# A fused four-block kernel: all four softplus in front of the scans and on VectorE, silus ahead of the last exponentials, first pair ahead in the norms

## What is computed

```python
x = x + _L0_conv_ref(_gn(x), ...)      # five steps of a diffusion
x = x + _L1_conv_ref(_gn(x), ...)      # 3x3 convolution
x = x + _L2_conv_ref(_gn(x), ...)      # layer norm, Mamba block, layer norm, projection
x = x + _L3_conv_ref(_gn(x))           # DCT

# inside _L2: mamba_block
xi, z = jnp.split(x @ in_proj_w.T, 2, axis=-1)
xs = silu(causal_conv(xi) + conv_b)
dt, Bm, Cm = jnp.split(xs @ x_proj_w.T, [dt_rank, dt_rank + d_state], axis=-1)
delta = softplus(dt @ dt_proj_w.T + dt_proj_b)
h = exp(delta * A) * h + (delta * xs) * B      # scan over 1024 pixels, per state
y = sum_n(h * C) + xs * D
y = y * silu(z)
```

## Time and profile before

| | us |
|---|---|
| median of 3 runs | 901.21 |
| lowest and highest | 901.0, 903.37 |
| the profiled execution's own time | 899.3 |
| its span | 897.5 |
| DVE busy | 792.5 (88%) |
| PE busy | 729.4 (81%) |
| ACT busy | 560.2 (62%) |
| POOL busy | 519.5 (58%) |

### The profile page before, as it was taken

How to read it: one execution, slowest core, us unless ns; L and a number is a source line. 1 busy time by engine, 2 the same in 40 slices (tenths; PEclk the granted TensorE clock), 3 DMA queues, 4 the chain that set the end, 5 groups by cost and what they waited for, 6 DMA issues and landing times.

```text
span 897.5 us, 10547 instructions
## 1 busy us (share of the span) xinstructions
PE 729.4 (81%) x3866; PEld 499.1 (56%) x3866; DVE 792.5 (88%) x682; ACT 560.2 (62%) x960; POOL 519.5 (58%) x243
## 2 busy tenths in 40 slices
PE   3898898977777678788799789988768677878896
PEld 2343343443677567778654434434338566777783
DVE  6979997769999998999969989775999999989984
ACT  2973342237669898979486724223684977897932
POOL 3104997121489697778510299912047979878851
PEclk9999999999789999999999999999988999999999
DMA  4002000000635355355200210000033445545431
GB/s 114 0 15 80 0 1 0 0 1 6 184 123 185 139 179 189 137 188 184 75 1 0 75 43 0 0 1 1 0 106 131 159 160 186 194 157 186 157 105 24
DMA packets 34066, 78.20 MB, mean 87 GB/s; under 512 B 15704, under 2 KB 15840, under 8 KB 34016
## 3 DMA queue, kind: packets, MB, share of 16 engines
q1 hardware_dynamic: 32608, 76.23, 25.3%
q0 software_dynamic: 320, 1.05, 0.5%
q10 hardware_dynamic: 1088, 0.26, 0.1%
HBM read 70.71 MB, written 2.62 MB: 82 GB/s over the span
## 4 chain that ended last, share of the span: by engine, by line
DVE 31%; PE 30%; ACT 20%; issue 13%; POOL 2%; DMA 1%; SPq 1%; DVEq 0%; POOLq 0%; ACTq 0%
ACT arena L958 15%; PE ps L749 7%; PE ps L510 6%; DVE arena L1775 6%; DVE ps L1766 5%; PE ps L549 4%; DVE HS L1775 3%; DVE arena L1730 3%; PE ps L763 2%; PE ps L641 2%; ACT ROWS L958 1%; ACT ps L958 1%; PE ps L600 1%; POOL arena L397 1%; PE ps L663 1%
## 5 line engine op out<-in xcount | busy, mean ns | idle before, releaser
L397 POOL TENSOR_TENSOR arena<-arena 128x1024 f32<-128x1024 f32 x85 | 200.3, 2368 | 60.9 <-DVE arena L1775 55.1
L958 ACT ACTIVATE arena<-arena 128x128 f32<-128x128 f32 (+3 forms) x412 | 157.0, 455 | 82.4 <-DVE arena L1669 64.7
L1775 DVE TENSOR_TENSOR_SCAN arena<-arena,ps 128x1024 f32<-128x1024 f32 x86 | 194.7, 2277 | 10.6 <-ACT arena L958 5.7
L958 ACT ACTIVATE arena<-arena,Amat 128x1024 f32<-128x1024 f32 x128 | 143.0, 1142 | 7.2 <-DVE arena L1775 6.0
L641 PE MATMUL ps<-mat,arena 128*128 128x128 f32 x1016 | 138.1, 281 | 5.5 <-POOL arena L397 5.0
L600 PE MATMUL ps<-mat,arena 128*128 128x128 f32 x560 | 82.2, 295 | 61.9 <-DVE arena L1775 35.9
L641 PEld LDWEIGHTS ps<-mat,arena 128*128 128x128 f32 x1016 | 119.7, 146 | 9.5 <-POOL arena L397 7.5
L397 POOL TENSOR_TENSOR arena<-HS,arena 128x1024 f32<-128x1024 f32 x42 | 99.6, 2370 | 30.1 <-DVE HS L1775 21.5
L749 PE MATMUL ps<-arena,mat 128*128 128x512 f32 x240 | 106.9, 595 | 9.4 <-DVE arena L1642 9.4
L600 PEld LDWEIGHTS ps<-mat,arena 128*128 128x128 f32 x560 | 66.8, 148 | 76.2 <-DVE arena L1775 45.3
L1775 DVE TENSOR_TENSOR_SCAN HS<-arena,ps 128x1024 f32<-128x1024 f32 x42 | 95.7, 2277 | 2.4 <-ACT arena L958 1.7
(11 more groups left out here) (219 smaller groups left out, 1321.8 us busy)
## 6 DMA issues: line engine op xcount, KB each, us to landing
arena<-c_rows SPq DMA_DIRECT2D x128, 512.0 KB, 3.9
arena<-arena SPq DMA_DIRECT2D x16, 252.0 KB
out<-arena SPq DMA_DIRECT2D x28, 64.0 KB, 2.4
xres<-x POOLq DMA_DIRECT2D x4, 256.0 KB, 5.4
xres<-x SPq DMA_DIRECT2D x4, 256.0 KB, 4.1
convw<-conv_w SPq DMA_DIRECT2D x1, 576.0 KB
c_rows<-ROWS SPq DMA_DIRECT2D x4, 128.0 KB, 1.9
mat<-mats SPq DMA_DIRECT2D x1, 448.0 KB, 3.9
```

The lines of the kernel that those rows point to most:

```text
L397: tt(HC[s % 2], HS[s % 3], CB[s % 4], ALU.mult).then_inc(S("hc"), 1)
L958: return nc.scalar.activation(out_, in_, func, bias=bias, scale=scale, accum_out=accum_out)
L1775: nc.vector.tensor_tensor_scan(HS[s % 3], DA[s % 3], PS[q][:, :], 0.0, ALU.mult, ALU.add).then_inc(S("scan"), 1)
```

## The change

- POOL: `relu_part` goes, all three of its calls a half.
- DVE: `relu_part(h, j)` takes the place of `first_relu_part` for all four images, and the semaphores are renumbered to suit. `normalize(0)` stands ahead of pair 1's statistics. `causal` takes a list of taps; `causal(0,0)` runs through, `variance(1)` behind it, two taps of `causal(0,1)` ahead of `normalize(1)` and two behind. `relu_x(1,1)`, `one_plus(3)` and `delta(3)` move in front of scan 0.
- PE: 14 spins behind the first group mean of the convolution. `xn_channels(0)` and `x_in_proj(0,0)` move ahead, the 4 spins between go. `dt_proj(0,0)` stands ahead of `xn_channels(1)`, and `z_in_proj(1,1)` and `dt_proj(1,1)` ahead of `bc_proj(0)`.
- ACT: `layer_scale(0)` ahead of `norm2(1)`, `abs_x(0,0)` ahead of `layer_scale(1)`. All silus stand ahead of `exp_of(2)`; `abs_x(1,1)` and `exp_of(3)` ahead of the logarithms, and the four logarithms stand together.

```diff
--- before.py
+++ after.py
@@ -379,12 +379,6 @@
 
-            def relu_part(h, j):
-                pool.wait_ge(S("sp"), 4 * h + j + 1)
-                pool.wait_ge(S(f"rx{j // 2}"), 2 * h + j % 2 + 1)
-                du = two_images(j, "DU")
-                tt(du, du, two_images(j, "DL"), ALU.subtract).then_inc(S("spw"), 1)
-
             def delta_u(h, j):
...
@@ -449,15 +443,11 @@
 
-                relu_part(h, 1)
-                relu_part(h, 2)
                 for s in range(SCANS):
...
                         delta_u(h, 1)
-                    if s == 5:
-                        relu_part(h, 3)
                     if s in (10, 25):
...
@@ -616,7 +606,7 @@
                 if j == 0:
-                    pe.wait_ge(S("first_du"), 2 * h + 2)
+                    pe.wait_ge(S("first_du"), h + 1)
                 else:
...
@@ -765,6 +755,7 @@
                 group_mean(D[0], h, 1, 0)
+                spin(PS[1], 14)
                 wino_product(h, 0, 0)
...
@@ -778,21 +769,22 @@
 
+                xn_channels(h, 0)
                 group_mean(D[1], h, 2, 1)
-                spin(PS[1], 4)
-                xn_channels(h, 0)
+                x_in_proj(h, 0, 0)
                 n2_pixels(h, 1)
-                x_in_proj(h, 0, 0)
                 z_in_proj(h, 0, 0)
                 x_in_proj(h, 0, 1)
+                dt_proj(h, 0, 0)
                 xn_channels(h, 1)
-                dt_proj(h, 0, 0)
                 x_in_proj(h, 1, 0)
...
                 z_in_proj(h, 0, 1)
+                z_in_proj(h, 1, 1)
+                dt_proj(h, 1, 1)
                 bc_proj(h, 0)
...
@@ -800,8 +792,6 @@
                 b_rows(h, 1)
-                z_in_proj(h, 1, 1)
-                dt_proj(h, 1, 1)
                 bc_proj(h, 1)
...
@@ -1309,35 +1299,35 @@
                 square(h, 0, 0)
+                layer_scale(h, 0)
                 norm2(h, 1)
-                layer_scale(h, 0)
                 square(h, 1, 0)
...
                 silu_x(h, 0, 0)
+                abs_x(h, 0, 0)
                 layer_scale(h, 1)
-                abs_x(h, 0, 0)
                 silu_x(h, 0, 1)
...
                 exp_of(h, 1)
+                abs_x(h, 1, 0)
                 silu_z(h, 0, 1)
-                abs_x(h, 1, 0)
+                silu_x(h, 1, 1)
+                silu_z(h, 1, 1)
                 exp_of(h, 2)
                 keep_rows(h, 0)
+                abs_x(h, 1, 1)
+                exp_of(h, 3)
                 ln_of(h, 0)
-                ln_of(h, 1)
                 keep_first_b(h)
-                ln_of(h, 2)
-                silu_x(h, 1, 1)
-                silu_z(h, 1, 1)
+                for j in range(1, 4):
+                    ln_of(h, j)
                 decay(h, 0)
...
                 keep_rows(h, 1)
-                abs_x(h, 1, 1)
                 decay(h, 2)
-                exp_of(h, 3)
                 decay(h, 3)
...
@@ -1355,8 +1345,6 @@
                         scaled_input(h, s + 3)
-                    if s == D_STATE - 1:
-                        ln_of(h, 3)
                     if h + 1 < HALVES:
...
@@ -1717,18 +1705,19 @@
 
-            def causal(h, k, b, first=True, rest=True):
+            def causal(h, k, b, some):
                 d, i = D[k], 2 * h + b
-                dve.wait_ge(S(f"xi{k}"), i + 1)
-                if b == 1:
-                    dve.wait_ge(S(f"xs{k}"), i)
                 w = [vecs[:, V_CONVW + t:V_CONVW + t + 1] for t in range(4)]
-                if first:
-                    ts(d["XI"], x_ps(k, b)[:, :], w[3], None, ALU.mult).then_inc(S(f"cconv{k}"), 1)
-                for t in range(1, 4) if rest else []:
-                    dve.wait_ge(S(f"cconv{k}"), 4 * i + t)
-                    stt(d["XI"][:, t:L], x_ps(k, b)[:, 0:L - t], w[3 - t], d["XI"][:, t:L], ALU.mult, ALU.add)\
-                        .then_inc(S(f"cconv{k}"), 1)
+                for t in some:
+                    if t == 0:
+                        dve.wait_ge(S(f"xi{k}"), i + 1)
+                        if b == 1:
+                            dve.wait_ge(S(f"xs{k}"), i)
+                        ts(d["XI"], x_ps(k, b)[:, :], w[3], None, ALU.mult).then_inc(S(f"cconv{k}"), 1)
+                    else:
+                        dve.wait_ge(S(f"cconv{k}"), 4 * i + t)
+                        stt(d["XI"][:, t:L], x_ps(k, b)[:, 0:L - t], w[3 - t], d["XI"][:, t:L], ALU.mult, ALU.add)\
+                            .then_inc(S(f"cconv{k}"), 1)
 
...
@@ -1743,17 +1732,14 @@
                 dve.wait_ge(S("ln"), 4 * h + j + 1)
-                if j == 0:
-                    dve.wait_ge(S("first_du"), 2 * h + 1)
-                else:
-                    dve.wait_ge(S("spw"), 3 * h + j)
+                dve.wait_ge(S("spw"), 4 * h + j + 1)
                 tt(two_images(j, "DL"), UU[j], two_images(j, "DU"), ALU.add).then_inc(S("delta"), 1)
 
-            def first_relu_part(h):
-                du = two_images(0, "DU")
-                dve.wait_ge(S("sp"), 4 * h + 1)
-                dve.wait_ge(S("rx0"), 2 * h + 1)
-                tt(du, du, two_images(0, "DL"), ALU.subtract).then_inc(S("first_du"), 1)
+            def relu_part(h, j):
+                du = two_images(j, "DU")
+                dve.wait_ge(S("sp"), 4 * h + j + 1)
+                dve.wait_ge(S(f"rx{j // 2}"), 2 * h + j % 2 + 1)
+                tt(du, du, two_images(j, "DL"), ALU.subtract).then_inc(S("spw"), 1)
 
...
@@ -1887,48 +1873,48 @@
                 add_conv(h, 1)
+                normalize(0, h, 0)
                 dve.wait_ge(S("X2"), 2 * h + 2)
                 stats(D[1]["X2"], D[1], h, 2, 1)
-                normalize(0, h, 0)
                 group_norm(D[1], h, 2, 1)
 
-                causal(h, 0, 0, rest=False)
+                causal(h, 0, 0, range(4))
                 variance(1, h, 0)
-                causal(h, 0, 0, first=False)
+                causal(h, 0, 1, range(2))
                 normalize(1, h, 0)
-                causal(h, 0, 1)
-                causal(h, 1, 0)
+                causal(h, 0, 1, range(2, 4))
                 relu_x(h, 0, 0)
+                causal(h, 1, 0, range(4))
                 relu_x(h, 0, 1)
-                causal(h, 1, 1)
+                causal(h, 1, 1, range(4))
+                relu_x(h, 1, 0)
                 one_plus(h, 0)
                 one_plus(h, 1)
-                first_relu_part(h)
-                relu_x(h, 1, 0)
+                relu_part(h, 0)
+                relu_part(h, 1)
                 one_plus(h, 2)
+                relu_x(h, 1, 1)
+                one_plus(h, 3)
+                relu_part(h, 2)
                 delta(h, 0)
                 first_delta_u(h)
+                relu_part(h, 3)
                 delta(h, 1)
-                dve.wait_ge(S("first_du"), 2 * h + 2)
+                dve.wait_ge(S("first_du"), h + 1)
                 scan_input(h, 0)
...
                 scan_input(h, 1)
-                scan_step(h, 0)
-                scan_step(h, 1)
-                relu_x(h, 1, 1)
-                scan_input(h, 2)
-                scan_step(h, 2)
-                one_plus(h, 3)
-
-                for s in range(3, SCANS):
+                delta(h, 3)
+                for s in range(2):
+                    scan_step(h, s)
+
+                for s in range(2, SCANS):
                     if s % D_STATE == 0:
...
                         gate(h, s // D_STATE - 1)
-                    if s == D_STATE + 1:
-                        delta(h, 3)
                     if s == 40:
...
```

## The result

| | before | after |
|---|---|---|
| median, us | 901.11 | 894.53 |
| lowest and highest | 899.17, 903.37 | 893.54, 896.67 |
| runs | 6 | 6 |
| span of the profiled run | 897.5 | 891.7 |
| DVE busy | 792.5 | 787.1 |

The ratio is 0.9928, with a 95% interval of 0.991 to 0.9946: 6.6 us faster, inside the range, and half of the 12.8 us of the sum. It is 4.4 us above the forecast of 890.1.

A forecast was written before the change was run, and what follows sets the result against it. DVE was taken to bound the kernel from the first causal step on. Gains less new waits, 8.05 us in the first half and 4.75 in the second, summed to 12.8 (888.4); PE's clock added 1.7: 890.1 us, range 885 to 897.5.

The forecast's parts named there:

- rival A: First scans lose their cover, DVE waits for PE at b_rows(4): 2.75 us a half, up to 897.3 us; chance 0.18.
- The spins: 14 spins ahead of the winograd products fill PE's gap and keep its clock up: gain 1.6 us a half.
- First pair ahead: In the norms, pair 0 goes ahead of pair 1's statistics: first causal step 3.85 us earlier.
- the walk: New order stepped through with the old rows' durations, giving start times and DVE's waits; scan 0 at 237.9 with spins.
- Work on DVE: Three relu parts add 3.4 us, instructions long beside POOL lose 6.3 (6.4): net 2.9 and 3.0 us less a half.
- wait (4): DVE waits 1.5 us at relu_x(1,1) for abs_x(1,1), behind a chain of PE projections, bc_proj(0) and keep_rows(0).
- Waits (1), (2) and (3): New DVE waits: 1.55 us for x_in_proj(0,1), 0.75 for x_in_proj(1,0), 0.1 at causal(1,1) behind silu_x(1,0).
- one of two halves is the likeliest: + 1.7: PE's 2.75 us gap ahead of wait (4)'s chain drops its clock in one half, moving 888.4 to 890.1 us.
- Rival B: Every PE gap is paid, five a half from silu_z to abs_x(1,1), 1.7 us each: 905.8 us; chance 0.06.
- ACT in the scans: Two table loads around ln_of(3) at step 15 go: DVE saves 2.5 us in the first half, nothing in the second.
- C: No change: work is only moved and DVE's long instructions stay long, leaving 901 us; chance 0.08.
- D: More than forecast: no cold gap, waits (1) and (4) half as long, 885.4 us; chance 0.08.

## Why the prediction was right, and where it wasn't

The measured 894.5 lies in the range, but outside the stretch of 888.4 to 891.8 that had the chance of 0.60. It lies in the one up to 897.3, which was there for rival A, and A's mechanism cost 0.31 us in one half of the profiled run. That the range reached so far is in part luck: it was drawn wide for a cost at the first scans, and a cost at the projections filled it.

**The spins.** Right. The winograd instructions fell to 5.39 us, the first causal step moved by the sum of this step and the next to 0.1 us in both halves. The size of 1.6 us a half is less sure: without the spins the trace has 2.35 us a half, and the medians 1.7 us for both halves together.

**First pair ahead.** Right: undone, it moved the first causal step by 3.8 us where 3.85 were named, and cost 5.1 us by the medians where the walk gives 5.2.

**Work on DVE.** Right as work, wrong as time. DVE's busy time fell by 5.4 us for the 5.9 of the two halves, and no softplus instruction was long any more. But this term was added in full, on the ground that DVE is the bound from the first causal step on. With the new order DVE waits at relu_x(1,1) for a chain of PE and ACT that doesn't depend on the relu parts in front of it, so that work taken off ahead of that wait only makes the wait longer. The relu parts put back on POOL showed that: relu_x(1,1) started after 22.50 us for 22.51. Only what was taken off behind that wait, 0.7 us there, was a gain. In the walk itself the starts were counted through, with wait (4) as a cost, which is why its 51.85 us held; what was wrong was to read the whole term as a gain of the softplus part.

**New waits.** Waits (1), (2) and (3) came out within 0.1 us where PE's clock held (1.47, 0.77 and none at causal(1,1)). Wait (4) was 1.70 where PE's clock held, for 1.5. Its cause, bc_proj(0) and keep_rows(0) in front of abs_x(1,1), was named, and the experiment that took keep_rows out of the way confirms it.

**PE's clock, the term that was mis-sized.** The step "one of two halves is the likeliest: + 1.7" failed twice. First in the number of places: I looked at the one gap of 2.75 us and left out the pair of 2.11 and 1.29 us ahead of x_in_proj(1,0), since a gap of 1.21 us had cost nothing; but this place, with 2.11 us idle ahead of the 1.09 us of transposes too, was followed by a slow projection in 13 halves of 16. Rival B had priced every gap and had the wrong picture too: not five gaps are paid a half, but one or two. Second in the price: I took 1.7 us from a place where two projections were slow, 3.27 and 2.23; here z_in_proj and dt_proj took 3.75 and 3.13, 3.05 too much, because the slow stretch covered both. The stretch from the first causal step to scan 0 was 3.25 us in the first half and 2.3 in the second above the walk; with the clock held it was still 0.25 above it (52.1 us), so that the clock's share is 3.0 and 2.05, some 5 us in place of 1.7. With all of it the sum is 12.8 - 5.55 = 7.25, which leaves 0.6 to the medians' 6.6.
What Part 1 of the Trainium skill's page TensorE: Matmul & The Clock Gate says, that equal kernels differ, is borne out: behind 2.85 to 2.94 us idle the projection was slow in 8 halves of 16, and the changed kernel run again had other slow projections. What its section HAM oscillation tells, that every burst behind a wait starts slow, isn't met at this gap: 8 of 16 didn't. But the waits of the kernel told of there are longer than this one. Behind the 4.04 us ahead of the winograd products, unfilled, the products were slow in all four halves.

**ACT in the scans.** Right where it was seen: at step 15 DVE no longer waits in the first half. From scan 3 on 4.4 us were gained for 4.9 and 2.1 for 2.6. In the first half a new wait of 0.76 us came at scan 19, at 299.7, behind two passes of ACT over the next half's input; in the second the 0.31 us at scan 4 is most of it. Neither wait was in the sum.

**Rivals.** A, the first scans: the scans 0 to 3 took 9.06 us for the walk's 9.05; in the second half the slow clock cost 0.31 us at scan 4 (680.88). The mechanism exists and is small (that wait was at most 0.73 us in the experiments), though by the letter of the prediction a wait of DVE for PE between scans 0 and 5 was a sign of being wrong. C and D didn't occur.

## What to carry to other kernels

Fill the idle time of TensorE ahead of a chain on which another engine waits, and count every gap on that chain, pairs of short ones with little work between them too: in this stage the gaps took back some 5 of the 12.8 us that the walk had found. Before adding up work taken off the busiest engine, find its next wait for another engine: what is removed ahead of that wait is worth nothing unless the wait goes too, and here two lines moved on ScalarE, which the profile shows busy for 62% of the span, brought nearly as much as the whole change. A walk through the new order with the old durations found each wait to 0.2 us where the clock held; it should then be used to ask which line would remove the wait, not only what the wait costs.

## What the runs showed that I had not expected

- Two gaps of 2.11 and 1.29 us with 1.09 us of transposes between them were followed by projections at 1.2 GHz in 13 of 16 halves, one gap of 2.86 us in 8 of 16. The counts are too small to call the first the worse of the two; that the shorter gaps aren't safe is shown.
- Of the 10 halves with a slow x_in_proj(1,0) and an unfilled gap ahead of z_in_proj(1,1), 4 had that one slow too; of the 6 in which x_in_proj(1,0) had run at full clock, 4. These are too few to say that the one bears on the other. With the first gap alone filled, z_in_proj(1,1) was slow in 2 halves of 4, so that this doesn't make the second gap safe.
- Without spins the same twelve winograd instructions behind the same 4.04 us took 7.09 us in both halves of one kernel and 7.76 and 7.74 in the other.
